# Gated recurrence, MLP and attention blocks on one core: the recurrence moved to VectorE, partition maxima to TensorE

## The reference

```python
def _wkv(w, u, k, v):                  # per channel, over t; p, q start at 0
    def step(carry, kv_t):
        p, q, o = carry
        kt, vt = kv_t
        no = jnp.maximum(o, u + kt)
        A = jnp.exp(o - no)
        E = jnp.exp(u + kt - no)
        y = (A * p + E * vt) / (A * q + E)
        no2 = jnp.maximum(w + o, kt)
        A2 = jnp.exp(w + o - no2)
        E2 = jnp.exp(kt - no2)
        return ((A2 * p + E2 * vt, A2 * q + E2, no2), y)
...
scale = jnp.clip(jnp.mean(jnp.abs(w_g), axis=-1, keepdims=True), 1e-08, None)   # ternary_quant, groups of 64
q = jnp.clip(jnp.round(w_g / scale), -1, 1)
...
scale = jnp.maximum(jnp.max(jnp.abs(x)) / FP8_MAX, SCALE_EPS)                   # _L1_ffn_ref
x_q = (x / scale).astype(jnp.float8_e4m3fn).astype(jnp.float32)
...
x = x + jnp.tanh(g_xattn[0]) * _L0_xattn_ref(16, 64, 256, L0_xattn_w, L0_xattn_u, _layernorm(x, axis=-1), ctx_2048)
x = x + jnp.tanh(g_ffn[0]) * _L0_ffn_ref(_layernorm(x, axis=-1), L0_ffn_w_gate_up, L0_ffn_w_proj)
x = x + jnp.tanh(g_xattn[1]) * _L1_xattn_ref(_layernorm(x, axis=-1), ctx_2048, mask_BxS2_bk0)
x = x + jnp.tanh(g_ffn[1]) * _L1_ffn_ref(_layernorm(x, axis=-1), L1_ffn_weight, L1_ffn_weight_scale, L1_ffn_bias)
```

## Time and profile before

| | |
|---|---|
| median of 3 runs | 175.67 us (175.4 to 177.21) |
| the profiled execution's own time | 175.69 us |
| its span, first to last instruction | 173.8 us |
| busy: PE, DVE, ACT, POOL | 119.8, 139.8, 74.3, 71.1 us |
| mean granted TensorE clock | 0.872 of full |

### The profile page before, as it was taken

How to read it: one execution, slowest core, us unless ns; L and a number is a source line. 1 busy time by engine, 2 the same in 40 slices (tenths; PEclk the granted TensorE clock), 3 DMA queues, 4 the chain that set the end, 5 groups by cost and what they waited for, 6 DMA issues and landing times.

```text
span 173.8 us, 2138 instructions
## 1 busy us (share of the span) xinstructions
PE 119.8 (69%) x726; PEld 77.6 (45%) x726; DVE 139.8 (80%) x269; ACT 74.3 (43%) x126; POOL 71.1 (41%) x85
## 2 busy tenths in 40 slices
PE   5649980781087970775895099979698857888462
...
GB/s 94 144 365 354 329 30 0 2 0 0 0 0 0 4 0 0 2 0 2 0 0 4 0 2 0 0 0 0 4 0 0 0 4 0 0 2 0 0 123 123
DMA packets 8045, 6.90 MB, mean 40 GB/s; under 512 B 2273, under 2 KB 7778, under 8 KB 8034
## 3 DMA queue, kind: packets, MB, share of 16 engines
...
q10 hardware_dynamic: 432, 0.00, 0.1%
...
## 4 chain that ended last, share of the span: by engine, by line
DVE 57%; issue 14%; PE 13%; DMA 6%; ACT 4%; POOL 3%; SPq 2%; POOLq 1%; DVEq 0%; ACTq 0%
DMA xs<-in_x_dram 6%; DVE xn L1010 5%; DVE GR L1124 5%; DVE stats L998 5%; DVE xs L1050 5%; DVE hbuf L1118 4%; DVE wsign L1094 4%; DVE wmask L1093 4%; DVE S L1020 3%; DVE wmask L1099 3%; DVE SV L1034 3%; PE ps L778 3%; PE ps L779 3%; PE ps L799 2%; DVE wmask L1100 2%
## 5 line engine op out<-in xcount | busy, mean ns | idle before, releaser
L778 PE MATMUL ps<-xhi,wT 128*128 128x512 f16 x64 | 25.7, 402 | 8.1 <-DVE wT L1084 5.7
L779 PE MATMUL ps<-xlo,wT 128*128 128x512 f16 x64 | 25.7, 402 | 0.0
L570 ACT ACTIVATE wgu_raw<-hbuf 128x512 f16<-128x512 f32 x16 | 10.0, 626 | 33.3 <-DVE hbuf L1118 33.2
L799 PE MATMUL ps<-wT,wgu_raw 128*128 128x256 bf16 x64 | 16.3, 294 | 6.5 <-DVE wT L1084 4.7
L998 DVE BATCH_NORM_STATS2 stats<-xs 128x6 f32<-128x256 f32 x32 | 12.2, 409 | 7.0 <-DMA xs<-in_x_dram 6.8
L1124 DVE TENSOR_TENSOR GR<-hbuf,wgu_raw 128x512 f16<-128x512 f32 x16 | 16.5, 1030 | 0.0
L799 PE MATMUL ps<-wT,GR 128*128 128x256 bf16 x64 | 16.2, 293 | 0.0
L1118 DVE SCALAR_TENSOR_TENSOR hbuf<-ps,pscale,sil 128x512 f32<-128x512 f32 x16 | 12.0, 747 | 5.1 <-PE ps L779 2.4
L439 POOL TENSOR_TENSOR sqsum<-sqsum,S 128x512 f32<-128x512 f32 x8 | 11.5, 1433 | 10.4 <-ACT S L573 10.1
L1010 DVE TENSOR_SCALAR xn<-xs,mv,rstd 128x256 f32<-128x256 f32 x24 | 13.7, 619 | 2.1 <-POOL rstd L368 2.1
L778 PEld LDWEIGHTS ps<-xhi,wT 128*128 128x128 bf16 x64 | 6.6, 102 | 18.7 <-DVE wT L1084 6.2
...
## 6 DMA issues: line engine op xcount, KB each, us to landing
...
mask_u<-in_mask_BxS_bk_dram SPq DMA_DIRECT2D x2, 32.0 KB, 7.4
```

The lines of the kernel that those rows point to most:

```text
L570: act.activation(hhi[:, h, j, :], hbuf[:, b, :], ACT.Copy).then_inc(hhi_ready, 1)
L778: pe.matmul(ps[:, 4 + 2 * b + up, :], w, xhi[:, h, c, :], start=(c == 0), stop=False)
L779: mm = pe.matmul(ps[:, 4 + 2 * b + up, :], w, xlo[:, h, c, :], start=False, stop=(c == CH - 1))
L799: mm = pe.matmul(ps[:, i // 2, o:o + C], part[:, h, j, i * P:(i + 1) * P], wp, start=(first and j == 0 and i % 2 == 0), stop=(not first an ...
```

## The change

- `Gs` and `R` become one tile `kv`, with rows of 65 places for 64 tokens: place 0 holds a zero, places 1 to 64 the exponential of the key (one ScalarE instruction for each piece instead of two). `kv[:, k, 1]` is key exponential times value, now multiplied on VectorE.
- The scans run over the padded rows (520 places) and give `sums`, whose places 0 to 63 are the sums up to the token before. The bonus is no longer in an exponential of its own: `gain` = exp(bonus), capped at both sides, is a factor for each channel, and one instruction for each of `den` and `y` computes `kv` times `gain` plus `sums`.
- `wkv_out` is one multiplication on VectorE, `y` times the inverse. GpSimd has no part in the recurrence. VectorE does the whole of pieces 2 and 3 ahead of the gate/up loop, where it had only their weights and denominators; inside the loop only `wkv_out(2)` and `wkv_out(3)` remain.
- `quant_sign` is one VectorE instruction on 32-bit words: `wT` and `sign_bits` (0x80008000), or `wmask`.
- The two maxima over partitions: TensorE transposes the broadcast column into PSUM (`spread_scales`, `spread_greatest`), VectorE takes the maximum along the row. `spread_scales` stands behind the transposes of block 2's input and ahead of `keep_warm`; `spread_greatest` stands behind the ten matmuls of `keep_warm(WARM_LAST, ...)`. The custom instructions on GpSimd are gone, and with them the library changes that stand around them in its queue.
- VectorE's queue has `weights_abs(3)` ahead of `quant_here_0(0)` instead of behind it.

```diff
-        GR = sb("GR", [P, 2, CHUNKS * CH, BPC, T])
-        Gs, R = GR[:, 0, :, :, :], GR[:, 1, :, :, :]
-        GV = sb("GV", [P, CHUNKS * CH, BPC, T])
...
+        dec = sb("dec", [P, CH, BPC * (T + 1)])
+        kv = sb("kv", [P, CHUNKS * CH, 2, BPC, T + 1])
+        sums = sb("sums", [P, CHUNKS * CH, 2, BPC, T + 1])
+        ratio = sb("ratio", [P, 2, CHUNKS * CH, CT])
+        den, y = ratio[:, 0, :, :], ratio[:, 1, :, :]
...
-            wkv_products(0)
-            wkv_products(1)
-            wkv_out(0)
-            wkv_out(1)
-            wkv_products(2)
-            wkv_products(3)
...
-            pool.wait_ge(gmax_ready, 1)
-            pool.partition_all_reduce(gmax_all[:, :], gmax[:, :], P, bass.bass_isa.ReduceOp.max).then_inc(gmax_done, 1)
...
-            pool.wait_ge(amax_ready, 1)
-            pool.partition_all_reduce(amax_all[:, :], amax1[:, :], P, bass.bass_isa.ReduceOp.max).then_inc(amax_done, 1)
...
-                    act.activation(Gs[:, k, :, 1:T], kps[:, :, 0:T - 1], ACT.Exp).then_inc(G_ready, 1)
-                    act.activation(R[:, k, :, 1:T], kps[:, :, 1:T], ACT.Exp, bias=bonus[:, c:c + 1]).then_inc(R_ready, 1)
+                    act.activation(kv[:, k, 0, :, 1:T + 1], kps, ACT.Exp).then_inc(G_ready, 1)
...
+            def spread_scales():
+
+                pe.wait_ge(gmax_ready, 1)
+                for g in range(2):
+                    t = pe.transpose(ps[:, 5, g * P:(g + 1) * P], gmax[:, g:g + 1].broadcast_to([P, P]), ident[:, :])
+                t.then_inc(gspread_ps, 1)
+
+            def spread_greatest():
+
+                pe.wait_ge(xn3T_ready, len(PARTS) * CH)
+                pe.wait_ge(amax_ready, 1)
+                pe.transpose(ps[:, 6, 0:P], amax1[:, :].broadcast_to([P, P]), ident[:, :]).then_inc(aspread_ps, 1)
...
+                    if n == 0 and up:
+
+                        pe.wait_ge(gmax_done, 1)
...
             keep_warm(WARM_LAST, 4, wT)
+            spread_greatest()
...
+            def wkv(k):
+
+                h, c = k // CH, k % CH
+                v = ctxT[:, c, h * CT:(h + 1) * CT].rearrange("p (b t) -> p b t", t=T)
+                dve.wait_ge(ctxT_ready, k + 1)
                 dve.wait_ge(G_ready, k + 1)
+                gv = step(dve.tensor_tensor(kv[:, k, 1, :, 1:T + 1], kv[:, k, 0, :, 1:T + 1], v, ALU.mult))
                 if k < CH:
                     dve.wait_ge(dec_ready, c + 1)
...
+                after(gv)
+                for w in range(2):
+                    scan = dve.tensor_tensor_scan(sums[:, k, w, :, :].rearrange("p b t -> p (b t)"), dec[:, c, :],
+                                                  kv[:, k, w, :, :].rearrange("p b t -> p (b t)"), 0.0, ALU.mult, ALU.add)
+                scan.then_inc(scan_ready, 1)
+                dve.wait_ge(scan_ready, k + 1)
+                for w in range(2):
+                    ins = dve.scalar_tensor_tensor(out=ratio[:, w, k, :].rearrange("p (b t) -> p b t", t=T),
+                                                   in0=kv[:, k, w, :, 1:T + 1], scalar=gain[:, c:c + 1],
+                                                   in1=sums[:, k, w, :, 0:T], op0=ALU.mult, op1=ALU.add)
+                    ins.then_inc(den_ready if w == 0 else Rv_ready, 1)
...
-                dve.tensor_scalar(wsign[:, b, :].bitcast(U16), wT[:, p, :].bitcast(U16), 0x8000, None,
-                                  ALU.bitwise_and).then_inc(wsign_ready, 1)
...
+                dve.scalar_tensor_tensor(out=wT[:, p, :].bitcast(U32), in0=wT[:, p, :].bitcast(U32), scalar=sign_bits[:, 0:1],
+                                         in1=wmask[:, b, :].bitcast(U32), op0=ALU.bitwise_and,
+                                         op1=ALU.bitwise_or).then_inc(wq_ready, 1)
...
             def power_of_two():
+                dve.wait_ge(gspread_ps, 1)
+                dve.tensor_reduce(gmax_all[:, :], ps[:, 5, 0:2 * P].rearrange("p (g n) -> p g n", g=2), AX_X,
+                                  ALU.max).then_inc(gmax_done, 1)
...
+            dve.wait_ge(aspread_ps, 1)
+            dve.tensor_reduce(amax_all[:, :], ps[:, 6, 0:P], AX_X, ALU.max).then_inc(amax_done, 1)
```

115 lines of the change are left out of this document (38 added, 77 removed).

## The result

The changed kernel takes 174.07 us (median of 20 runs, 172.13 to 175.79), the kernel before 176.06 us beside it (20 runs, 175.35 to 177.8). The ratio is 0.985, 95% interval 0.982 to 0.988: 1.5% faster, 2.7 us (2.0 by the medians). The ratio leaves out the slower executions, four of the changed kernel's twenty, and the medians take in all. Forecast were 172.8 us and a range of 169.8 to 175.7, against an own time of 175.69 us, a ratio of 0.984 to that. The profiled execution took 174.68 us, with a span of 172.9 us (before: 173.8).

A forecast was written before the change was run, and what follows sets the result against it. VectorE's queue was taken to bound the kernel up to 103 us. From 175.69 us, -4.6 in front and +1.8 at the end gave 172.9, forecast as 172.8 us since the median stands 0.02 lower; range 169.8 to 175.7.

The forecast's parts named there:

- The sum in front: VectorE's queue up to 103 us: stalls, recurrence, mask, bias, signs and new waits together -4.6 us.
- a piece of the recurrence: VectorE's recurrence work: each piece with its output costs 5.01 us instead of 3.71; four pieces +5.2 us.
- the mask: GpSimd's two mask operations, now near 24 us beside VectorE's recurrence, stall VectorE: +1.0 us (0 to 1.3).
- the bias: GpSimd's `bias_g`, moved to about 41 us between quantization operations, stalls VectorE: +0.4 us (0 to 0.8).
- a sign: VectorE's sign on 32-bit words, six times: each saves 0.44 us, -2.6; rival, not cheaper: +0.5, 175.9 us, chance 0.06.
- the stalls of the twelve operations: VectorE instructions lengthened beside GpSimd's twelve recurrence operations return to normal: -10.5 us; rival, stalls not returned: chance 0.06.
- the reduction of the first maximum: VectorE's 0.42 us reduction from PSUM ahead of the first `ffn_mul`: 0, hidden by `gate_up(0)`.
- The lock: VectorE instructions and GpSimd operations on SBUF exclude each other; the later waits for the whole of the other.
- The new waits: VectorE waits for ScalarE's copies before `weights_abs(2)` and `weights_abs(3)`, 1.1 and 0.85 us: +1.9 us (0 to 2.5).
- The clock rival: TensorE idles some 1.9 us ahead of `gate_up(0)`, its clock falls to 1.2 GHz: +1.7, 174.5 us, chance 0.20.
- The second maximum: At the end: transpose behind filler matmuls +1.5, last-quarter wait gone -0.77, one VectorE stall: +1.8 us (+0.7 to +2.9).
- The estimate by the rule of the Trainium skill: At the end, each of two remaining GpSimd operations holds VectorE once: +2.9 us there, 173.9 us in all.

The follow-up runs named there:

- the idle products: The changed kernel with twelve GpSimd multiplications of a scratch tile, results unused, where the kernel before had its twelve recurrence operations: 180.95 us, ratio 1.028 to the kernel before.
- the run with sixteen fillers: The changed kernel with sixteen filler matmuls instead of eight ahead of the first gate products: 171.97 us, ratio 0.976 to the kernel before.
- the second profile of the changed one: Profile from measuring the changed kernel once more, unchanged: 173.02 us, ratio 0.978 to the kernel before.

## Why the prediction was right

**The sum in front held in its busy time, nearly term by term.** VectorE's busy time up to the start of the second half's `xlo`, in the kernel before and the changed one (columns as in the earlier trace rows; the third busy time is VectorE's):

```profile
0.00:103.15 103.15, 65.22 (x348) 40.69 (x348) 88.78 (x153) 43.19 (x67) 45.31 (x56) 0.79 0.18 56
```

```profile
0.00:98.81 98.81, 62.95 (x346) 41.21 (x350) 82.05 (x159) 41.26 (x63) 28.79 (x41) 0.82 0.19 59
```

It is 6.7 us less. The terms of the prediction that are busy time (-10.5 + 5.2 + 1.0 + 0.4 - 2.6) give -6.5. Singly: a piece of the recurrence is 4.46 us from start to start and its output 0.62, together 5.08 where 5.01 was forecast; the mask cost 0.53 us (1.0), the bias 0.16 (0.4), a sign is 0.75 us long and 0.67 from start to start, 0.40 less than the pair before where 0.44 was forecast, so -2.4. With 5.5 for the recurrence, 0.53, 0.16 and -2.4, what remains for the stalls of the twelve operations is 10.5 us, the sum over the ten stretched groups. That closes only to about half a microsecond: the reduction of the first maximum adds 0.42 us of busy time, and the bias held up an instruction by 0.16 us before the change as well. Counted directly, the time by which VectorE's instructions up to this mark are longer than their like is 18.3 us before and 7.7 us with the change, 10.7 less. The 7.7 us are mask and bias, 0.7, and 7.0 us beside the work that GpSimd kept (the sums of squares and the linear weights; the first such is 1.64 us for 0.69, at 68.57 us), which the prediction doesn't mention.

**The lock** is shown, not only argued: twelve operations of GpSimd for which nobody waits cost 7.9 us. That is less than the 10.5 us of the kernel before; the idle products take 1.1 to 1.2 us alone, and they fall beside other instructions. The size depends on what lies beside (that the two differ for this reason is argued, not shown).

**The new waits** are 1.99 us where 1.95 was worked out; 0.41 of them stood there before, which I had not taken off. Whether they cost the time that they last is less sure: filled, they brought 0.7 or 0.85 us at the first gate product and 1.4 at `xlo` against the profile with the same clock, and nothing that the times can tell.

**The clock rival happened.** The prediction's main case had `gate_up(0)` at full clock, and gave a chance of 0.20 to the fall ahead of it. The changed order leaves TensorE 2.1 to 3.5 us without work there, not the 1.9 us that I worked out, and each profile with eight fillers shows the fall. Its price on VectorE was 1.1 us of waiting more (2.32 for 1.26); the run with sixteen fillers puts it at 1.5 us at the first `hbuf` and 1.6 at `xlo` and at the end, profiles with the same later falls compared, where I had 1.7. That the mark at `xlo` was still right, -4.3 for -4.6, has three small reasons: 0.2 us more of busy time gone, 1.6 us more of these waits where I had 1.9, and 0.3 us less of VectorE's other idle time, with no one place for it. That is luck: a term which the main case put at nothing was made good by small errors the other way.

The ratio, too, is right partly by luck. The ratio forecast (0.984) lies between those measured (0.985 and 0.978), but between the profiles the gain is 0.9 us, and 1.8 in the second, where 2.8 was forecast. The forecast started from an execution of 175.69 us; beside the runs here the kernel before had medians of 176.1 to 176.7 us.

**The second maximum** was right in kind: the transpose is behind the filler matmuls, the scale comes 1.4 us later than before (5.05 for 3.67 us behind the last maximum; +1.5 forecast). Mis-sized was the stall: the wait for the last quarter went (-0.77), but two roundings are held up, not one (1.7 us for 1.05). TensorE's clock also falls behind the 4 us without work, so that its first 24 matmuls take 4.45 us, but it then waits 1.06 us for VectorE, and without the fall 18.1 + 1.4 - 0.8 + 1.7 already gives 20.4 us from the last maximum to the end, for the 20.2 measured. Together the tail costs 2.1 us by the profiles and 2.4 by experiment, for the +1.8 forecast.

The estimate by the rule of the Trainium skill ("SBUF — State Buffer", "Who interferes with whom") was +2.9 us for the tail. The trace has the two stalls that this rule wants, each 0.85 us, not the whole length of GpSimd's operation (1.67 and 1.16 us). It fits the rule all the same: the two roundings begin 0.70 and 0.11 us behind GpSimd's operations and end 0.16 and 0.55 us behind their ends, so each is held until GpSimd is done.

**The middle** had no term. In the first profile the clock stood at 0.50 for 3.4 us from 137.6 us on, and 1.1 of the 1.3 us lie there: from the second mean square (`msq`) behind the loop to the scores (`sc`) it is 10.6 us for 9.5. Of the thirteen profiles without fillers there six have this fall and take 10.1 to 10.6 us for this part, seven, the kernel before and the second profile of the changed one among them, don't and take 9.5. What decides it is open: the gaps ahead of it are alike in all of them (1.1 and 0.7 us), and the one run with fillers there kept its clock, which proves little, since seven kept it without.

**The 32-bit sign** needed its own run most: with the old one the rest of the change, its tail included, is worth nothing (1.004). Its 2.4 us by the trace are 3.8 by the medians; the difference is open.
